# Graph layers on one core: edge phases without loops, a second product buffer, experts' rows asked for first

## The reference, cut to what matters

```python
x = x + L0_gnn(layernorm(x))   # attention, 8 heads of 32, keys and values of the source node
x = x + L0_ffn(layernorm(x))   # 8 experts, top 2
x = x + L1_gnn(layernorm(x))   # graph attention, 4 heads of 64
x = x + L1_ffn(layernorm(x))   # 8 experts of width 1024, top 1 with a capacity

# the part of both gnn's that the change touches
score = sum(q[dst] * k[src])        # L0; in L1: leaky_relu(e_src[src] + e_dst[dst])
ex    = exp(score - segment_max(score, dst)[dst])
out   = segment_sum(ex / segment_sum(ex, dst)[dst] * v[src], dst)
```

## Time and profile before

| | before |
|---|---|
| median of 3 runs | 9977.47 us |
| the profiled execution, its own time | 9991.05 us |
| its span, first to last instruction | 9989.3 us |
| mean granted TensorE clock | 0.794 |
| `att` edge phase | about 537 to 3965 us of the span |
| `gat_att` edge phase | about 5490 to 8700 us |
| switch_experts | about 8950 to 9840 us |

### The profile page before, as it was taken

The page is one execution under the profiler, slowest core; times in us unless marked ns, Lnnn a source line. Parts: engine busy times, 40 slices in busy tenths (PEclk is TensorE's granted clock), DMA queues, the critical chain, the costliest instruction groups (busy, mean ns, idle before and its releaser), DMA issues. The chain is left out here.

```text
span 9989.3 us, 143724 instructions
## 1 busy us (share of the span) xinstructions
PE 7296.0 (73%) x33600; PEld 5271.7 (53%) x33600; DVE 5876.5 (59%) x16050; ACT 3420.6 (34%) x10075; POOL 4441.4 (44%) x4446
## 2 busy tenths in 40 slices
PE   3877887887888788535955677777777777659993
PEld 2555555555555555334743444545445545458873
DVE  3467777777777777752124555555555555663332
ACT  1256555555565564222422111111111111222220
POOL 2045555555555553052034655655555556440004
PEclk6989889888898888757977666766676766759996
DMA  4455555555555554444345333333333333335555
GB/s 142 159 151 154 148 153 151 146 151 148 152 153 149 149 151 132 140 144 132 119 143 170 86 81 81 82 81 82 83 82 82 82 82 82 78 118 178 178 178 160
DMA packets 814099, 1276.19 MB, mean 128 GB/s; under 512 B 274566, under 2 KB 585110, under 8 KB 812734
## 3 DMA queue, kind: packets, MB, share of 16 engines
q0 software_dynamic: 272448, 833.22, 30.5%
q1 hardware_dynamic: 540755, 432.95, 14.5%
HBM read 1070.02 MB, written 211.92 MB: 128 GB/s over the span
## 5 line engine op out<-in xcount | busy, mean ns | idle before, releaser
L694 POOL DMA_INDIRECT att_kv<-kv,att_idx x1872 | 1850.1, 988 | 1912.3 <-issue 1475.6
L694 POOL DMA_INDIRECT gat_att_vst<-ft,gat_att_idx x1872 | 1877.6, 1003 | 1340.6 <-DVE gat_att_score L956 723.7
L772 PE MATMUL gat_att_pag<-gat_att_msg,gat_att_S 128*128 128x260 f32 x3744 | 1466.6, 531 | 31.1 <-DVE gat_att_msg L978 9.1
L730 PE MATMUL att_pqd<-sum_acc,att_ST 128*128 x3744 | 1136.1, 431 | 390.9 <-ACT att_ST L816 295.5
L772 PE MATMUL att_pag<-att_msg,att_S 128*128 128x264 f32 x3744 | 1160.5, 436 | 84.4 <-DVE att_msg L978 42.4
L730 PEld LDWEIGHTS att_pqd<-sum_acc,att_ST 128*128 128x128 f32 x3744 | 769.6, 214 | 602.2 <-issue 480.5
L772 PEld LDWEIGHTS gat_att_pag<-gat_att_msg,gat_att_S 128*128 128x128 f32 x3744 | 888.2, 263 | 347.2 <-issue 153.4
L816 ACT CAST gat_att_ST<-gat_att_pST 128x256 bf16<-128x256 f32 x936 | 348.1, 372 | 2110.3 <-remote 1032.9
L772 PEld LDWEIGHTS att_pag<-att_msg,att_S 128*128 128x128 f32 x3744 | 692.6, 206 | 372.6 <-issue 166.9
L727 PE MATMUL gat_att_pqd<-sum_ed,gat_att_ST 128*128 x5616 | 372.1, 171 | 634.0 <-ACT gat_att_ST L816 436.9
L727 PEld LDWEIGHTS gat_att_pqd<-sum_ed,gat_att_ST 128*128 128x128 bf16 x5616 | 335.5, 106 | 941.3 <-issue 860.8
(11 more groups left out here) (474 smaller groups left out, 11913.9 us busy)
## 6 DMA issues: line engine op xcount, KB each, us to landing
sexp_w<-in_L_ffn_w_dram SPq DMA_DIRECT2D x112, 1024.0 KB
att_kv<-kv,att_idx POOLq DMA_INDIRECT x1872
gat_att_vst<-ft,gat_att_idx POOLq DMA_INDIRECT x1872
top_row<-tok SPq DMA_DIRECT2D x106, 256.0 KB
ytok<-top_y SPq DMA_DIRECT2D x106, 256.0 KB
kv<-qkv_row SPq DMA_DIRECT2D x50, 520.0 KB
sexp_row<-stok SPq DMA_DIRECT2D x56, 260.0 KB
sy<-sexp_y SPq DMA_DIRECT2D x56, 256.0 KB
```

The costliest lines, as they stand in the source:

```text
L694: pool.indirect_dma_start(row, None, rows_t, IndirectOffsetOnAxis(ap=idx[:, k, 2 * p + i:2 * p + i + 1], axis=0)).then_inc(s_g[p % R], 16)
L730: t = pe.matmul(pqd[p % 2][:, i * D:i * D + D], lhs, acc[:, bass.ds(b + 1, 1), 0:D], start=True, stop=True)
L772: t = pe.matmul(pag[p % 2][:, 0:AW], S[:, gs % RG, 2 * p + i, :], msg[:, p % 2, i, :], start=(i == 0), stop=(i == 1))
```

## The change

- `run` in edge_phase calls `step` for all 119 groups with plain numbers; the loop goes. Both phases and all five engines are touched. What `step` does for a group is the same.
- `prod` gets a second buffer, used by the pair's parity; products of pair T waits for T - 1 reductions. It is in `att` alone.
- In switch_experts the request for the rows of tile i+4 stands ahead of that for the weights of tile i+3.

```diff
-    UN, HEAD = 18, 8
...
-        prod = None if gat else m.sb("prod", [P, 2 * D])
+        prod = None if gat else m.sb("prod", [P, 2, 2 * D])
...
         def run(eng, step):
 
-            assert (NG - 1 - HEAD) % UN == 0
-            for g in range(HEAD):
-                step(g, g)
-            with eng.Fori(0, (NG - 1 - HEAD) // UN) as it:
-                for j in range(UN):
-                    step(it * UN + (HEAD + j), HEAD + UN + j)
-            for g in range(NG - 1, NG + 2):
+            for g in range(NG + 2):
                 step(g, g)
...
-                        wait(v, s_score, T)
-                        v.tensor_tensor(prod[:, :].rearrange("p (i d) -> p i d", i=2), kv[:, p % R, :, 0:D],
+                        wait(v, s_score, T - 1)
+                        v.tensor_tensor(prod[:, p % 2, :].rearrange("p (i d) -> p i d", i=2), kv[:, p % R, :, 0:D],
...
-                                    prod[:, :].rearrange("p (i h o) -> p i h o", i=2, h=H),
+                                    prod[:, p % 2, :].rearrange("p (i h o) -> p i h o", i=2, h=H),
...
                     sp.wait_ge(s_y, i + 1)
+                    if i + R < TILES:
+                        rows(i + R)
                     if i + WR < TILES:
                         weights(i + WR)
-                    if i + R < TILES:
-                        rows(i + R)
```

## The result

| | before | after |
|---|---|---|
| median of 5 runs each | 9977.47 us | 9913.24 us (9885.65 to 9927.57) |
| ratio, 95% interval | | 0.9934 [0.9917, 0.9951] |
| the profiled execution, its own time | 9991.05 us | 9923.58 us |
| mean granted TensorE clock | 0.794 | 0.798 |
| `att`, first to last instruction | 3407.9 us | 3314.5 us, 93 less |

What follows compares the result with a forecast made beforehand. Edge phases were taken as relays between engines with dense stretches where VectorE is full, switch_experts as TensorE-busy; 50 + 30 + 80 + 14 = 174 us off 9991.05 gave 9817, on the median's footing 9803, range 9690 to 9920.

Steps and rivals of the forecast that it cites:

- now the weights do: L = 10.6: switch_experts: with rows first, weights land last, y to hidden falls from 11.1 to 10.6 us, 14 us gained.
- the prediction's own formula: switch_experts: the period closes over three tiles, 3P = L + P + hidden 7.07 + result 7.07 + y 5.5.
- a loss of 20: switch_experts, rows first: worst end of its range, if weights come 0.7 us later than hidden began.
- 541 x 0.18 = 97: `att`, second buffer: 541 direct hand-overs where VectorE had not sat idle long, 0.18 us each; 80 of 97 taken.
- Rival 2: `att`: second buffer gives nothing, gathers or TensorE set the dense stretches; 94 us off, 9883; chance 0.12.
- Rival 1: Edge phases: only the loop's returns count, register work is hidden everywhere; 106 us off in all, 9871; chance 0.22.
- `gat_att` moving by less than 10 us: `gat_att`: the prediction's stated sign that its reasoning is wrong and rival 1 holds.
- The comparison of the earlier trace: Written-out groups against loop groups before the change: 0.69 us a group in `att`, 0.90 in `gat_att`; 50 and 30 us taken.
- the 160 forecast: Edge changes: constant waits 50 us in `att` and 30 in `gat_att`, second product buffer 80.
- Rival 4: `att`: TensorE idles more and its granted clock falls below 0.85; at 0.80 100 us slower, 10078; chance 0.06.

Runs made afterwards that it cites:

- x7: Kernel before plus both edge changes, weights' order kept, rows asked for by ScalarE on its own queue: 9740.74 us, ratio 0.9863.
- w1: Kernel before with two 64-byte transfers issued ahead of each weights request, old order kept: 9913.6 us, ratio 1.0048.
- x4: Kernel before with only the loop written out, one product buffer, quick chip: 8496.34 us, ratio 0.9920.
- x2: Changed kernel with the old order in switch_experts (both edge changes), quick chip: 8396.4 us, ratio 0.9800 to the kernel before.
- y4: Kernel before with both phases written out, one product buffer, slow chip: 9889.96 us, ratio 0.9901.
- y2: Changed kernel with the old order in switch_experts (both edge changes), slow chip: 9884.4 us, ratio 0.9880 to the kernel before.
- y1: Kernel before itself, unchanged, run for a trace on a slow chip: 10002.87 us, ratio 0.9997.
- z3: Kernel before with three extra index loads per weights request, absent from the trace, so the same program, quick chip: 8568.2 us, ratio 0.9997.

## Why the prediction was right or wrong

**The order: sign wrong, and this is the step that failed.** It stood as "now the weights do: L = 10.6". The rows did get out of the way, and the weights were named rightly as what is late next. But they were taken to land when the rows did before, as if one queue lands the same bytes at the same time in either order, though the prediction itself had them asked for 0.7 us later and behind 260 KB. The 0.7 stood in its text and not in its L. The weights land 12.14 us after y, 1.96 later than before and 1.26 later than the last rows did. Of the 1.96, 0.84 is the request's own delay. Some of the rest is the rows' transfer beside them (x7: 0.63 later with the weights asked for as early as ever). x7 also shows the premise itself: with no request behind the other's all had landed at 10.81, where before it was 10.88. Then the request for B2 holds SyncE for 4.7 us instead of 3.1. These requests, before and then after (ns minimum/median/maximum):

```profile
L2440 SPq DMA_DIRECT2D sexp_b<-in_L_ffn_b_dram x56: 2575/3102/4624, 8953.6 to 9804.7; - x56
```

```profile
L2433 SPq DMA_DIRECT2D sexp_b<-in_L_ffn_b_dram x56: 2701/4716/5242, 8850.8 to 9740.1; - x56
```

The remaining 0.5 us or so was not separated; whether the longer hold makes it was not tested. The working also had no term for the clock, though a rival had one for `att`. TensorE waits longer once a tile, the clock granted to the stage goes from 0.98 to 0.97, and hidden takes 7.49 us where it took 7.15. With both terms the prediction's own formula holds: 2P = L + hidden + 7.07 + 5.5 = 12.62 + 7.49 + 12.57 gives P = 16.34, and the trace has 16.32. w1 shows it without bytes: 0.87 us of issue time ahead, and the period is 0.96 longer; hidden is 0.44 longer at a granted clock of 0.96, so by the formula about a quarter of the loss is the clock's. The lower end of the range for this part, a loss of 20, was passed, too.

**The second buffer: mechanism right, size a matter of the chip.** The hand-over went from 0.10 us behind to 0.08 ahead, the pair from 2.41 to 2.21 us. Alone it brought 24 us and 53 us where 80 were forecast. The failed step is "541 x 0.18 = 97", of which 80 were kept: it counted hand-overs by VectorE's own waits. The gap went at three direct hand-overs a group (positions 4 to 6), and on the slow chip time won there came back elsewhere. On top of the written-out loop, by the traces of `att`, it is worth 99 us on the quick chip (x4 to x2) and 32 on the slow one (y4 to y2). Rival 2 (it gives nothing) was nearer than the forecast on the slow chip, though not for the gathers as far as the view names them: after, the waits for `att_kv` before products sum to 27.3 us of the phase. The answer for the tile `att_prod` of the kernel after (who ended VectorE's idle time before products, us, times):

```profile
  issue: 187.3, 163
  DMA att_kv<-kv,att_idx: 27.3, 26
  PE att_pqd L723: 8.1, 5
```

**The loop: sum about right, and the cause differs by chip.** 80 us were forecast for both phases, 50 of them in `att`, 30 in `gat_att`, and only 12 of the sum for returns, since the earlier trace rows showed 0.8 us at a return. Written out alone it brought 67 on the quick chip and 99 to 113 on the slow one. On the slow chip the traces have 59 and 33, and at most 2.5 us a return, so the forecast's split held in sign and near enough in size. How near is partly luck: the groups there differ from one to the next by 1.5 to 2.4 us, and two executions of the kernel before, and y1, differ by some 20 us in each phase. On the quick chip it went another way: 26 in `att`, mostly the returns (5 of 7.4, 37) less the slower steady groups (15), and 47 in `gat_att`, nearly all of it the shorter gathers. That 12 ends at 5.8 us make 69, as much as x4's 67, is thus a coincidence. Rival 1 (only the returns count) was right of `att` on the quick chip alone, and lacked the price. Its sign, `gat_att` moving by less than 10 us, came true (9), but with 20 us between two executions of one kernel it could tell nothing. It had its rule from the Trainium skill ("Runtime: NRT & Kernel Launch", Instruction fetch mechanics): sequential fetch is mostly hidden, and a taken branch to a page not held stalls the engine. The runs on the quick chip agree in sign and in order: in `att` a return costs 7.4 us with a body of 18 groups and 3.8 with one of 6, where the instruction queues move 558 packets instead of 896. Why the same return shows 0.5 to 2.5 us on the slow chips stays open. The comparison of the earlier trace rows, groups 2 to 7 against the rest, gave 28.23, and y4 has 28.22; that of the earlier trace rows gave 0.90 us where y4 has 0.31 and the change 0.12.

**In the first comparison** the edge changes thus gained 93 + 9 = 102 of the 160 forecast, on the chip with a ratio of 0.9880 119, on the quick one 168. The rest of the miss is the order's 50 us. The 9913 lies in the range, 9690 to 9920, but by 7 us and not for a reason that the range was made of, since the order lost more than its worst end. Rival 4 (the clock falls in `att`) did not happen: 0.89 as before.

**Why chips differ.** TensorE and ScalarE hand a pair back and forth, and on the slow chips TensorE's results come late: of its expands, turns and aggregates some 30 to 40% are announced over 1.5 us after their modelled end in the kernel before, on the quick chip 0 to 7%. The granted clock differs, too: in the loop groups of `att` it is 0.99 on the quick chip and 0.89 in the earlier trace rows. The page's groups of expand, on the chip of y1 and on the quick one (z3), show it as TensorE's idle time behind the copy that needs the previous turn:

```profile
L730 PE MATMUL att_pqd<-sum_acc,att_ST 128*128 x3744 | 1124.3, 428 | 364.6 <-ACT att_ST L816 266.8
```

```profile
L730 PE MATMUL att_pqd<-sum_acc,att_ST 128*128 x3744 | 993.1, 388 | 39.1 <-DVE att_prod L962 20.7
```

365 us against 39, for one program. That a faster VectorE gains less with that wait in the way is an argument; no run shows it. What makes these results late, and whether the lower clock is its cause or its consequence, was not found and stays open. The 48 us that the two edge changes bring together beyond their sum on the quick chip lie in the steady groups of `att`: the second buffer takes 0.44 us off a group in the loop (23.29 to 22.85) and 1.06 off one written out (23.43 to 22.37), and 0.62 x 108 is 67 us. Why the loop's groups take only part of it stays open.

## What to carry to other kernels

When a request is moved ahead of another in one queue, add up all that the second then bears: its own issue, the bytes ahead, the longer hold of later requests, and the clock that TensorE loses while it waits. A deeper ring for the cheap transfer frees its time without delaying the dear one, and here it turned a loss of 36 us in the stage into a gain of 30. The price of a loop's return depends on the body and on the chip: read it where groups are steady, over all returns and against the spread of other groups, and check it by changing the number of rounds. When two parts of a change fit the total, look at each phase before believing it: here 12 x 5.8 us fitted, and over half of the gain was elsewhere.

## What was not expected of the hardware

- One program takes 8564 us on one chip and 9873 to 10003 on others, with TensorE's idle time before expand at 39 and 365 us.
- In `att`, which five engines run in step, a return of the loop cost 7.4 us on the quick chip with 18 groups in the body and 3.8 with 6, and 0.5 to 2.5 us on the slow chips.
- With waits and addresses as constants GpSimd's mean gather in `gat_att` went from 1032 to 1007 ns on the quick chip, which is the 47 us that the phase gained.
- A request that holds SyncE for 3.1 us holds it for 4.7 when one of 260 KB was issued ahead of the same tile's weights, and stays at 3.1 behind two of 64 bytes.
- 0.87 us of issue time a tile, with no bytes, cost 38 us over 56 tiles, and the mean hidden matmul took 398 ns, where it takes 381 to 388 in the traces without it.
